# A fused gated feed-forward kernel on one core: a three-part bfloat16 split moved ahead of a register read, and a first group in another order

## The reference, cut to what matters

```
x = L0_attn_x                                   # (2, 2048, 1024) float32: 4096 tokens
xn = layernorm(x)                               # over the last axis
s = attention_like(xn)                          # autocorrelation by FFT, its top 6 lags, softmax,
                                                # sum of xn rolled by these lags
def qlora(x, wq, A, B):
    return x @ tile(wq, (1, 4)).T + (x @ A.T @ B.T) * 0.5      # rank 2
gate = silu(qlora(xn, w1q, a1, b1))             # 1024 -> 2752
up = qlora(xn, w3q, a3, b3)
g = silu(qlora(gate * up, w2q, a2, b2))         # 2752 -> 1024
out = x + s * g
```

## Time and profile before

| what | value |
|---|---|
| runs (median, lowest, highest) | 854.31, 854.24, 854.91 us |
| the profiled execution's own time | 854.79 us |
| its span, first to last instruction | 853.0 us |
| mean granted PE clock | 0.997 |
| busy PE / DVE / ACT / POOL | 831.5 / 576.9 / 331.5 / 147.5 us |

### The profile page before, as it was taken

The page is one execution under the profiler, slowest core; times in us unless marked ns, Lnnn a source line. Parts: engine busy times, 40 slices in busy tenths (PEclk is TensorE's granted clock), DMA queues, the critical chain, the costliest instruction groups (busy, mean ns, idle before and its releaser), DMA issues.

```text
span 853.0 us, 11238 instructions
## 1 busy us (share of the span) xinstructions
PE 831.5 (97%) x4200; PEld 441.9 (52%) x4200; DVE 576.9 (68%) x941; ACT 331.5 (39%) x544; POOL 147.5 (17%) x238
## 2 busy tenths in 40 slices
PE   6989999999999999999999999999999999999997
PEld 4434575335744367434763347534575336744366
DVE  6877734686766775688667776678766696744535
ACT  5986635434133342333423332333323434122231
POOL 5242102222012220122201230023201222000000
PEclk9999999999999999999999999999999999999999
DMA  9630026000230003200042000501014000220004
GB/s 294 251 118 25 26 109 214 25 26 25 100 124 26 25 26 124 100 25 25 27 152 71 26 32 19 198 26 49 26 51 173 25 1 0 100 99 1 1 2 148
DMA packets 18903, 62.13 MB, mean 73 GB/s; under 512 B 2464, under 2 KB 4224, under 8 KB 18576
## 3 DMA queue, kind: packets, MB, share of 16 engines
q1 hardware_dynamic: 18832, 61.28, 20.9%
HBM read 44.49 MB, written 16.78 MB: 72 GB/s over the span
## 4 chain that ended last, share of the span: by engine, by line
PE 69%; DVE 14%; ACT 6%; issue 6%; DVEq 3%; POOL 1%; DMA 1%; SPq 0%; ACTq 0%; POOLq 0%
PE g L1238 23%; PE u L1238 22%; PE zb L1382 4%; DVE junk L798 4%; PE g L1274 3%; PE g L1441 2%; PE u L1441 2%; PE u L1450 2%; PE g L1448 2%; PE u L1448 2%; PE g L1450 2%; DVEq L857 1%; ACT sil L540 1%; DVE h L841 1%; DVE xt L1110 1%
## 5 line engine op out<-in xcount | busy, mean ns | idle before, releaser
L540 ACT ACTIVATE sil<-g,winv 128x512 f32<-128x512 f32 (+1 forms) x176 | 119.9, 683 | 269.5 <-PE g L1274 241.3
L841 DVE SCALAR_TENSOR_TENSOR h<-u,winv,sil 128x512 f32<-128x512 f32 x168 | 125.7, 749 | 123.1 <-ACT sil L540 107.9
L1238 PE MATMUL g<-xt,w_h 128*128 128x512 f16 x656 | 196.3, 381 | 0.0
L1238 PE MATMUL u<-xt,w_h 128*128 128x512 f16 x656 | 195.2, 379 | 0.0
L1238 PE MATMUL g<-xt,w_l 128*128 128x512 f16 x328 | 124.4, 379 | 0.0
L1238 PE MATMUL u<-xt,w_l 128*128 128x512 f16 x328 | 124.4, 379 | 0.0
L798 DVE CUSTOM_DVE_ANT_0 junk<-xn,abc 128x1024 bf16<-128x1024 f32 x96 | 120.3, 1253 | 6.0 <-issue 2.7
L1238 PEld LDWEIGHTS u<-xt,w_h 128*128 128x128 f16 x656 | 64.1, 98 | 77.5
L1238 PEld LDWEIGHTS g<-xt,w_h 128*128 128x128 f16 x656 | 55.5, 98 | 83.7 <-issue 32.0
L447 POOL TENSOR_TENSOR ve<-mv,three 128x1 f32<-128x1 f32 x30 | 6.0, 201 | 473.0 <-DVE mv L780 473.0
L540 ACT ACTIVATE gg<-g 128x512 f32<-128x512 f32 x32 | 19.1, 597 | 148.4 <-PE g L1444 72.5
(11 more groups left out here) (261 smaller groups left out, 1132.5 us busy)
## 6 DMA issues: line engine op xcount, KB each, us to landing
xr<-in_x SPq DMA_DIRECT2D x32, 512.0 KB, 4.6
out_x<-ob SPq DMA_DIRECT2D x31, 512.0 KB, 2.9
xf<-in_x SPq DMA_DIRECT2D x30, 512.0 KB, 3.3
raw_w<-in_w2t SPq DMA_DIRECT2D x1, 2560.0 KB
abc<-in_a SPq DMA_DIRECT2D x1, 2048.0 KB, 8.1
raw_w<-in_w1t SPq DMA_DIRECT2D x2, 768.0 KB, 7.8
raw_w<-in_w3t SPq DMA_DIRECT2D x2, 768.0 KB, 9.1
raw_w<-in_w1t SPq DMA_DIRECT2D x1, 704.0 KB, 12.7
```

What stands on the lines that cost most here:

```text
L540: return nc.scalar.activation(out, in_, f, **kw)
L841: stt(out=h[0:n, p % NH, :], in0=up, scalar=winv[0:n, 3 * block_of(p) + 1:3 * block_of(p) + 2], in1=sil[0:n, p % 2, :], op0=ALU.mult, op1= ...
L1238: o = mm(bank[:], a, x, start=opens and t == 0, stop=closes and t == len(terms) - 1)
```

## The change

The split of the next group's low-rank input stands ahead of the flag in groups 1 to 6, where it stood behind tile 0 (and, in the rare arm, ahead of it). In the first group, ahead of chunk 0: the second square sum stands ahead of the second half's copies; the first sum over partitions goes to another bank (`mb`); the first high part stands ahead of two quarter normalisations; `z0(1)` is issued within chunk 0; chunk 0's gate takes its low-weight terms ahead of its low-input terms. The raw differences wait for `zst` and not for the low weights. In the chunks, `far_lags` of group 0 come later and in the order of the tiles, the second cast and step of b one chunk sooner and ahead of other work of their chunk, the high parts of block 3 two chunks later, low parts of block 3 in chunks 11 and 12, the second and third statistics and the second normalisation of group 1 one chunk later, and `b_scale(3)` one chunk later.

```
-        STATS_AT = [(3, 6, 9, 13)] + ...
-        NORM_AT = [(5, 8, 12, 16)] + ...
+        STATS_AT = [(3, 7, 10, 13)] + ...
+        NORM_AT = [(5, 9, 12, 16)] + ...
-        FAR_AT = [(7, 10, 14, 18)] + [(4, 10, 16)] * (NG - 1)
-        FAR0_AT = (2, 3, 4, 6)
+        FAR_AT = [(8, 11, 14, 18)] + [(4, 10, 16)] * (NG - 1)
+        FAR0_AT = (5, 6, 7, 9)
-        HIGH_AT = {..., 8: ((3, 0),), 9: ((3, 1),)}
+        HIGH_AT = {..., 10: ((3, 0),), 11: ((3, 1),)}
-                  10: ((3, 0, 0),), 11: ((3, 0, 1),), 12: ((3, 1, 0), (3, 1, 1))}
-        CAST_AT, STEP_AT, B_AT = {4: 0, 7: 1}, {5: 0, 8: 1}, {2: 1, 9: 2, 12: 3}
+                  11: ((3, 0, 0), (3, 0, 1)), 12: ((3, 1, 0), (3, 1, 1))}
+        CAST_AT, STEP_AT, B_AT = {4: 0, 6: 1}, {5: 0, 7: 1}, {2: 1, 9: 2, 13: 3}
 gpsimd
-            pool.wait_ge(wl_done, 4)
+            pool.wait_ge(zst_done, 1)
             for q in FIRST_DIFF:
                 raw_difference(q)
 scalar
             quarter_normal(1)
+            w_bound(0, 1)
             x_copy(1, 0)
-            w_bound(0, 1)
             x_copy(1, 1)
+            w_high(0, 0)
             quarter_normal(2)
             quarter_normal(3)
-            w_high(0, 0)
...
-                        if p in CAST_AT:
-                            b_cast(1, CAST_AT[p])
                         if p in B_AT:
                             b_scale(B_AT[p])
                         for b, m in BOUND_AT.get(p, ()):
                             w_bound(b, m)
+                        if p in CAST_AT:
+                            b_cast(1, CAST_AT[p])
 vector
-            w_scale(0, 1, gb[0][:, 0:3])
+            w_scale(0, 1, mb[:, 0:3])
             x_copy(2)
             x_copy(3)
             w_low(0, 0, 0)
+            w_low(0, 0, 1)
             xt_low(0, 0)
             xt_low(0, 1)
-            w_low(0, 0, 1)
...
+                        if p in STEP_AT:
+                            b_step(1, STEP_AT[p])
                         for b, m, k in LOW_AT.get(p, ()):
                             w_low(b, m, k)
                         if p in W2L_AT:
                             w2_low(W2L_AT[p])
-                        if p in STEP_AT:
-                            b_step(1, STEP_AT[p])
...
                     if not last:
                         last_projections(i + 1)
+                        z_split()
                     flag(i)
                 drain()
                 rare = dve.value_load(some[0:1, 0:1])
                 with dve.If(rare > 0):
-                    if i and not last:
-                        z_split()
...
                         else:
                             multiply(i, q)
                             add_input(i, q)
-                        if i and not last and q == 0:
-                            z_split()
 tensor
+                if p == m == 0:
+                    lower(0)
+                    lower(1)
+                    crossed(0)
+                    crossed(1)
+                    return
...
                 if fresh:
+                    if p == 0:
+                        pe.wait_ge(xa_done, 6)
+                        pe.wait_ge(xd_done, 2)
+                        z0(1)
                     first_chain(gb[p % 3], 0, p)
...
-            pe.wait_ge(xa_done, 5)
-            scale_sum(0, gb[0], 0)
+            scale_sum(0, mb, 0)
             pe.wait_ge(dev_done, 12)
+            pe.wait_ge(wall_read, 1)
             for q in range(4):
                 o = nc.tensor.transpose(mb[:, q * P:(q + 1) * P], rs[:, q:q + 1].broadcast_to([P, P]), ident[:])
             o.then_inc(rsb_ready, 1)
             for q in range(2, 4):
                 quarter_across(q)
-            pe.wait_ge(xa_done, 6)
-            pe.wait_ge(xd_done, 2)
-            z0(1)
```

More of the change, by code:

```diff
@@ L303, in at_group @@
             return i * per + n
-        STATS_AT = [(3, 6, 9, 13)] + [(1, 7, 13, 19)] * (NG - 1)
-        NORM_AT = [(5, 8, 12, 16)] + [(2, 8, 14, 20)] * (NG - 1)
+        STATS_AT = [(3, 7, 10, 13)] + [(1, 7, 13, 19)] * (NG - 1)
+        NORM_AT = [(5, 9, 12, 16)] + [(2, 8, 14, 20)] * (NG - 1)
         Z_AT = [{}] + [{3 + 6 * q + r: (q, r) for q in range(3) for r in range(4)}] * (NG - 1)
@@ L333, in build @@
         BOUND_AT = {2: ((2, 0),), 3: ((2, 1), (3, 0)), 4: ((3, 1),)}
-        HIGH_AT = {1: ((1, 0), (1, 1)), 5: ((2, 0),), 6: ((2, 1),), 8: ((3, 0),), 9: ((3, 1),)}
+        HIGH_AT = {1: ((1, 0), (1, 1)), 5: ((2, 0),), 6: ((2, 1),), 10: ((3, 0),), 11: ((3, 1),)}
         LOW_AT = {1: ((1, 0, 0), (1, 0, 1)), 2: ((1, 1, 0), (1, 1, 1)),
                   6: ((2, 0, 0), (2, 0, 1)), 7: ((2, 1, 0), (2, 1, 1)),
-                  10: ((3, 0, 0),), 11: ((3, 0, 1),), 12: ((3, 1, 0), (3, 1, 1))}
-        CAST_AT, STEP_AT, B_AT = {4: 0, 7: 1}, {5: 0, 8: 1}, {2: 1, 9: 2, 12: 3}
+                  11: ((3, 0, 0), (3, 0, 1)), 12: ((3, 1, 0), (3, 1, 1))}
+        CAST_AT, STEP_AT, B_AT = {4: 0, 6: 1}, {5: 0, 7: 1}, {2: 1, 9: 2, 13: 3}
         W2_AT = {13: 0, 15: 1, 16: 2, 18: 3, 19: 4, 20: 5}
@@ L496, in sums @@
                 tt(xq4[:, q, :], yh[:, 0:DQ], yh[:, DQ:HALF], ALU.add).then_inc(sum_done, 1)
-                pool.wait_ge(far_done, n - 3 if i > 1 else FIRST_DIFF.index(q) + 1)
+                pool.wait_ge(far_done, n - 3)
                 tt(dd[:, q, :], xn[:, 0:DQ], xn[:, HALF:HALF + DQ], ALU.subtract).then_inc(diff_done, 1)
@@ L523, in _ @@
             pool.wait_ge(a2_done, 3)
-            pool.wait_ge(zst_done, 1)
             nc.gpsimd.memset(hf_l[64:P, HN, :].bitcast(F32), 0.0).then_inc(zeroed, 1)
@@ L740, in _ @@
                     if i == 0 and p in FAR0_AT:
-                        far_lags(0, FIRST_DIFF[FAR0_AT.index(p)])
+                        far_lags(0, FAR0_AT.index(p))
                     if not last and p in NORM_AT[i]:
@@ L1248, in first_chain, with crossed @@
                     mm(bank[:], wt_h[m][:, k, c:c + P], xt[:, k, :], start=k == 0, stop=False)
-                for k in range(2):
+                def crossed(k):
                     if p == m == 0:
@@ L1252, in first_chain, with lower @@
                     mm(bank[:], wt_h[m][:, k, c:c + P], xt[:, 2 + k, :], start=False, stop=False)
-                if p == 0 and m:
-                    z0_spread()
-                for k in range(2):
+                def lower(k):
                     pe.wait_ge(wl_done, 4 * b + 2 * m + k + 1)
                     mm(bank[:], wt_l[m][:, k, c:c + P], xt[:, k, :], start=False, stop=False)
+                if p == m == 0:
[4 more added lines that the diff above has]
+                    return
+                crossed(0)
+                crossed(1)
+                if p == 0:
+                    z0_spread()
+                lower(0)
+                lower(1)
             def bank_free(i, p):
```

## The result

The changed kernel takes 858.59 us (median of 6 runs, 856.82 to 860.83), the kernel before, beside it, 854.27 us (853.75 to 854.91). The ratio is 1.005, with a 95% interval of 1.0031 to 1.0069: slower by 4.3 us by the medians, with a loss of 2.6 to 5.9 us in the interval. I had predicted 857.5, between 854.8 and 859.8.

A forecast was written before the change was run, and what follows sets the result against it. PE was taken as the bound, busy 831.5 of 853.0 us, so only its waits count. Group ends +4.4 and first group -1.2 give +3.2 us on the 854.31 median: 857.5, range 854.8 to 859.8.

The forecast's parts named there:

- The ends, +4.4 us: Ends of groups 1 to 6: PE waits 1.25 us for ACT instead of 0.5 for `zs`, each end 0.74 us later.
- The two conditions: What `down(i, 3)` waits for at a group's end: `zs` from DVE, and ACT's reading of tile 1's banks (`gg`).
- a break-even of 1.24: Group ends: work ahead of the flag costs time only beyond a 1.24 us shift; `z_split` is 0.74 us over.
- The stretch hangs on the load and the branch: DVE, group ends: the 3.35 us between flag and tile 0's `multiply` moves with the flag and absorbs no shift.
- The rival that began with it: Group ends: the stretch ends on its own time, so the `zs` wait goes and none replaces it; 848.0 us, chance 0.10.
- The waits for `gg`, 7.5 us in all: Ends of groups 1 to 6: six waits of `down`'s matmuls for ACT's `gg`, about 1.25 us each.
- The first group, -1.2 us: Start to chunk 12: PE reaches chunk 12 near 64.4 instead of 65.65; bounds -2.4 and +0.5 us.
- My +0.45 at `lora`: Ahead of chunk 0: reordering costs 0.65 us at `z0(1)`, partly at half clock, carried as +0.45 us to chunk 1's `lora`.
- Both old waits: First group: 1.26 of the 1.68 us wait for the last square sum won; the wait at 62.28 for `bst` goes.
- the late statistics at chunk 11: First group: `stats(1, 1)` slips from 53.02 to near 56.7, delaying ACT's second normalisation and chunk 11's transposes.
- The differences behind `zst`: First group: `zst`'s last step, 1208 ns beside POOL's differences, regains 0.46 us; counted as zero, bounds -0.3 and 0.
- The loss weighed for the low parts of block 1: Chunk 4: moved differences and copies might hold up these low parts by about 0.5 us; one way to the upper bound.

The follow-up runs named there:

- Experiment 1: Kernel before with only the split moved ahead of the flag, first group as before: 859.48 us against 854.77, ratio 1.0052.
- experiment 3: Kernel before with PE's transposes of `zs` moved behind the first two weight slices of `down(i, 3)`, split behind tile 0: 849.23 us against 854.77.
- experiment 5: Changed kernel (split ahead of the flag) with PE's transposes of `zs` moved into `down(i, 3)`: 862.11 us against 854.32 for the kernel before.
- experiment 8: Kernel before with the split cut in two, five steps ahead of the flag, six casts left behind tile 0: 853.12 us against 854.32.
- experiment 9: Kernel before without the register load, branch and general path: 847.74 us against 854.30, ratio 0.9923.
- experiment 10: Kernel before without register load, branch and general path, and with the split ahead of the flag: 847.76 us against 854.30, ratio 0.9922.
- experiment 12: The changed kernel measured again, for its clock: 859.58 us against 854.30 for the kernel before, ratio 1.0057.
- experiment 2: Changed kernel with the split put back behind tile 0, the first group's new order alone: 853.43 us against 854.77 for the kernel before.
- experiment 4: Kernel before with the first group's new order and the transposes of `zs` inside `down(i, 3)`, split behind tile 0: 849.79 us against 854.77.
- experiment 6: Kernel before with the new order ahead of chunk 0 alone, old chunk tables and split's place: 855.01 us against 854.32, ratio 1.0004.
- experiment 7: Kernel before with the new tables and orders of the chunks alone: 853.38 us against 854.32, ratio 0.9985.
- experiment 11: Kernel before with the new chunk tables and the transposes of `zs` inside `down(i, 3)`, head and split as before: 847.91 us against 854.30.

## Why the prediction was right, step by step

- **The ends, +4.4 us: right in mechanism and place; the size came out in part by luck.** The wait for `zs` went, a wait for `gg` came, 1.19 us where 1.25 was worked out, and group 1's end is 0.70 us later for 0.74. Over six ends it is 3.7 us in the profiles, not 4.4. Experiment 1 isolates the part at +4.7, but its profile has 1.5 us of half clock in it that the sum had nowhere. The sum took every end like group 1's, whose wait for `zs` (0.52 us) is the shortest of the six; 7.5 us of new waits less the 5.1 of rows 2 would have been 2.4, so the two figures of the prediction did not go together. The two conditions are shown by experiments 3 and 5 (one edit, with opposite signs depending on which condition binds) and by 8, where a shift of 1.25 us (the flag at 220.61, the last dot product's read at 219.36) costs nothing, as a break-even of 1.24 says.
- **"The stretch hangs on the load and the branch": right.** It moved with the flag unchanged (3.34 us), and experiments 9 and 10, without load, branch and general path, have none. The rival that began with it fell: no run shows its 848.0 with the split early and the branch in place.
- **The waits for `gg`, 7.5 us in all: mis-sized.** They measured 8.6. I took the stretch as 3.35 us at every end, but it has a longer case: 4.44 us at group 5's end in the changed kernel, and 4.09 at group 3's in the kernel before. One end waits 2.29 us. Every kernel with the split ahead of the flag and the branch in place repeats this at group 5 (experiments 1, 5 and 12, 4.44 to 4.53 us), and those with the whole split behind tile 0 at group 3 (experiments 2, 3, 4, 6, 7 and 11, 4.06 to 4.32), so it is bound to a place in the code and not to chance.
- **The clock: missing from the term of the ends.** I looked for it ahead of chunk 0 only. Experiments 1 and 5 show it fallen behind the longest of the waits. The shortest run of the changed kernel is 3.1 us over the shortest before (856.82 against 853.75), its three long ones 5.5 to 6.6 over the median before. So the forecast of 857.5 lies close to the median of 858.59 because two faults offset each other: the sum of the profiled parts is +1.9 and not +3.2, and the clock adds what no term of it has.
- **The first group, -1.2 us: about right, for partly other reasons.** The trace has -1.8, of which 0.6 lie ahead of `lora` of chunk 1 and are not shown to be the order's; experiment 2's medians have -1.3. `z0(1)` at 19.11 was foretold as 19.2. My +0.45 at `lora` took the half clock for granted. With it, `lora` stands at 28.41, as before (28.46), so the reordering itself costs nothing there. Without it, it is 0.6 us sooner in the first profile, but at 28.51 in experiment 6's, which starts later, and experiment 6 finds no gain in the median. From `lora` of chunk 1 to chunk 12 the sum was -1.65; the profile has 36.03 us for 65.65 - 28.46 = 37.19, that is -1.16. Both old waits went as said. Of the new ones, 0.44 us ahead of chunk 8's square (I had 0.75) and 1.06 behind the late statistics at chunk 11, for which the prediction printed no price; its steps leave 0.38 for it.
- **The differences behind `zst`: as the row said.** `zst`'s last step takes 747 ns where it took 1208, and PE waited for it neither time. The loss weighed for the low parts of block 1 did not come: their two rows take 1.95 and 1.95 us where they took 1.95 and 1.94. The differences now fall on the small steps of block 1's scale, of which two take 0.27 and 0.61 us where they took 0.17 each, and the low parts still start 0.6 us sooner (31.03 for 31.64).

## What to carry to other kernels

Before moving work out of a wait, list every condition of the waiting instruction with its time: the second one was met only 0.47 us ahead of PE's arrival, and 1.98 us of work put ahead of it made it the bound. Ask first whether the consumer can ask later: moving four transposes by 2.8 us on PE won 5.5 us, where moving the split on DVE lost 4.7. Work ahead of a register load and branch delays all that is behind it, so what the next engine waits for should come first.

## What the runs showed of the hardware

- A register load and a taken branch on DVE left 3.3 to 3.7 us without an instruction at most ends of groups 1 to 6 (3.6 to 3.8 at group 0's), and 4.1 to 4.5 us at one end of the kernel before, of the changed one and of experiments 1 to 7, 11 and 12; in experiment 8 none is over 3.64. Without them the next instruction started 0.07 us after the one before had (experiment 9). The load itself took 0.30 to 0.54 us. The Trainium skill, page Runtime: NRT & Kernel Launch, section Instruction fetch mechanics, says that a taken branch to a target outside the window in the instruction memory has to fetch it first; it gives no time for it. The traces agree: in the twelve profiles with the branch, the instruction queue q14 moved one packet of 8 KB within the stretch at each of the 73 ends of groups 0 to 6 that have a short one, and two packets at each of the 11 that have a long one. No experiment separates the fetch from the load and the `drain` ahead of it.
- A single wait of PE of 2.3 us was followed by half clock for 3.4 us in one profile (experiment 1), one of 2.8 us in another (experiment 5), and one of 2.3 us in two profiles by none (the changed kernel, both times). In experiment 1 it cost 1.5 us more than the wait's own length. Waits of 1.2 to 1.7 us at the group ends were in no profile followed by it.
